# A two-layer adaLN transformer on one core: the expert stage with another order on TensorE, VectorE and GpSimd, GpSimd's own Newton steps, four sum and two output buffers

## The chip, the cores and the metric

One NeuronCore of a Trainium2 chip (trn2) runs the whole program. The metric is the device time of one execution in microseconds (us), the median of several runs; lower is better.

## What is computed

Two transformer layers with adaptive layer norm on x [8, 512, 256]. The change touches the last stage alone, in which the second layer's attention output is projected and normed and goes through a block of eight experts. Cut to that stage, with m the modulation rows (`ga`, `sb`, `cb`, `gb`) of a batch element:

```python
proj = (einsum('bhtk,hkd->bhtd', out_norm, Wo) + bo) * clip(gate, 0, 1)   # out_norm: by head
x = x + ga * proj.sum(axis=1) / H
h = layernorm(x) * (1 + cb) + sb
# the expert block, on h as [4096, 256]
x_attn = (layernorm(h) * ln_g + ln_b) @ attn_w + attn_b + h
g = x_attn.reshape(2, 8, 256, 256)                    # expert e takes 2 x 256 tokens
a = gelu(einsum('metd,edf->metf', g, w1) + b1)        # 256 -> 1024
y = einsum('metf,efd->metd', a, w2) + b2              # 1024 -> 256
x = x + gb * gelu(y @ next_w + next_b)
```

Every product is made from float16 halves: a high half and a low half of each operand, three matmuls for one product.

## The kernel before

The program has stages one after the other: attention and MLP of layer one, attention of layer two, and the stage of the change, `experts` (tile names with `D_`). It treats eight experts of 512 tokens each. Every engine walks the same list of ten bodies (`bodies`): body b works on three experts at once, e = b + 1 (projection of the attention output, sum, both norms), a = b (gate and the first expert product) and m = b - 1 (second expert product, last product, output). Engines take their instructions in the order in which the code writes them; between engines stand semaphores.

The names, in the order in which an expert goes through them:

- `project` (TensorE) multiplies yh, yl by the attention output weights into X; VectorE scales that into the sum buffer x3 (L2086), GpSimd adds the input rows x2t (L1860). x3 has three buffers, taken in turn.
- `statistics` (VectorE) takes mean and variance of the 512 tokens into mv and ve. `root_of` makes rstd = 1/sqrt(ve): a first guess r0 on GpSimd by the power -0.5 (L1845) and one Newton step, three instructions on VectorE (L2050, L2052, L2055). There are two roots for each expert: one for ht (L2094, L2099, four passes each), one for xn (L2108, four passes).
- `turn` (TensorE) transposes ht and xn through X. ScalarE copies them out (hTb, h2h), VectorE makes the low half h2l (L2119).
- `gate` (TensorE, 12 matmuls) multiplies h2h, h2l by attn_w; VectorE adds hTb (gf, L2074), ScalarE makes gh, GpSimd the low half gl (L1853).
- `first` (TensorE, s = 0 to 7, 6 matmuls each) fills PA; ScalarE makes af and Hh of it, VectorE the low half Hl (L2065, `splits`).
- `second` (TensorE, four chunks c of 12 matmuls) fills PW. ScalarE makes y2f and y2h, GpSimd y2l (L1865). `last` is the last product; ScalarE's gelu writes it to the output buffer xo (one buffer, the tile `last`), GpSimd's `finish` (L1835, L1838) multiplies by gb and adds x3, SyncE stores it.
- `weights` makes the float16 halves of an expert's weights, eh on ScalarE and el on VectorE (L2034), in two halves of w_st; half 0 is w1, half 1 is w2. SyncE loads the next half when the el of the one before is made. `prepare` makes yh (ScalarE) and yl (GpSimd, L1827) of the expert after next.

On TensorE body b issues: second(c=0), gate, second(c=1), project(q=0), second(c=2), project(q=1), second(c=3), first(0, 1), last, first(2, 3, 4), turn of ht, first(5, 6, 7), turn of xn. All matmuls of the expert products and the gate have one line, L2148; those of `project` and `last` have L2156 and L2160, the transposes L2207.

Of the kernel before, what the change touches and what calls it, by code (L numbers as in the profile page):

```python
# [21 lines left out]
TT = T // 128  # L22
# [1218 lines left out]
def mlp0(nc, d, keep, stay):  # L1241

    table = mlp_slots()
    with ExitStack() as ctx:
# [11 lines left out]
        ve, lnr, rstd = stay("ve", [128, TT]), stay("lnr", [128, 3, TT]), stay("rstd", [128, TT])  # L1256
        off = {"w1": 0, "w2": FT * HID, "h1": 2 * FT * HID, "h2": (2 * FT + HM) * HID, "w3": (2 * FT + 2 * HM) * HID}
# [415 lines left out]
def experts(nc, d, keep):  # L1673

    NA = HM
    with ExitStack() as ctx:
# [24 lines left out]
        x3 = [sb(f"x3{k}", [128, TT, C]) for k in range(3)]  # L1701
# [12 lines left out]
        xo = by_token(keep["last"])  # L1714
# [19 lines left out]
        n_mm, of_s, og_s, x4_s, o_st = sem("n_mm"), sem("of"), sem("og"), sem("x4"), sem("o_st")  # L1734
# [13 lines left out]
        def _(sp):  # L1748
# [46 lines left out]

            def body(b, e, a, m):
                n = b + 2
                if n < E8:
                    if n >= 2:
                        load_x(n)  # L1800
                    if n % 2 == 0 and n >= 4:
                        load_rows(n // 2)
                    load_w(n, 0)
                if m is not None:
                    q0, q1, t_ = halves(m)
                    for q_, q in enumerate((q0, q1)):
                        sp.wait_ge(x4_s, 2 * m + q_ + 1)
                        sp.dma_start(d["out"][q, t_, :].rearrange("(t p) c -> p t c", p=128),
                                     xo[:, 2 * q_:2 * q_ + 2, :]).then_inc(o_st, 16)
                if n < E8:  # L1810
                    load_w(n, 1)

            bodies(body)
            sp.wait_ge(o_st, 32 * E8)

        @block.gpsimd
        def _(pool):
# [12 lines left out]
            def finish(m):  # L1830

                for q in range(2):
                    v = xo[:, 2 * q:2 * q + 2, :]
# [4 lines left out]
                    nc.gpsimd.tensor_tensor(v, v, x3[m % 3][:, 2 * q:2 * q + 2, :], ALU.add).then_inc(x4_s, 1)  # L1838

            def root_of(nth):  # L1840

                pool.wait_ge(ve_s, nth + 1)
                if nth >= 1:
                    pool.wait_ge(newton, 3 * nth)
                nc.gpsimd.tensor_tensor(r0[:, :], ve[:, :], power[:, :], ALU.pow).then_inc(guess, 1)  # L1845

            prepare(0)

            def body(b, e, a, m):
# [26 lines left out]
        def _(act):  # L1876
# [58 lines left out]
            def body(b, e, a, m):  # L1935
# [52 lines left out]
        def _(dve):  # L1988
# [49 lines left out]
            def statistics(src, nth, ready):  # L2038
# [10 lines left out]
                dve.wait_ge(guess, nth + 1)  # L2049
# [288 lines left out]
```

## Time and profile before

| | us |
|---|---|
| median of 3 runs | 2118.07 |
| lowest and highest | 2112.24, 2121.11 |
| the profiled execution, its own time | 2117.34 |
| its span, first to last instruction | 2115.6 |
| PE (TensorE matmul) busy | 1862.5 (88%) |
| DVE (VectorE) busy | 1341.4 (63%) |
| ACT (ScalarE) busy | 1209.5 (57%) |
| POOL (GpSimd) busy | 577.1 (27%) |

The expert stage is the last sixth of the span. Moments in the trace are us from the span's start. "Busy" of PE overstates, since matmuls are pipelined and their records overlap. In a row of the timeline the first number is the start, the second how long the instruction or the merged run took; what stands in brackets is how long the engine had been idle before it and which instruction ended that.

### The profile page before, as it was taken

How to read it: one execution, taken by the hardware profiler on the slowest of the kernel's cores; microseconds unless marked ns; L12 is line 12 of the kernel's file. 1: busy time of each engine (PE TensorE's matmuls, PEld its weight loads, DVE VectorE, ACT ScalarE, POOL GpSimd, SP SyncE). 2: the span in 40 equal slices, each digit the busy share in tenths (PEclk: the TensorE clock that was granted, in tenths of full speed). 3: DMA queues.
4: the chain of work that ended last, by engine and by line, in shares of the span. 5: the costliest groups of instructions: out<-in, count | busy, mean ns of one | idle time of the engine just before them, and what ended most of it. 6: DMA issues, size and time to landing. Idle time of an engine off the chain costs nothing. (4 is left out here: it accounts for less than half of the span.)

```text
span 2115.6 us, 29755 instructions
## 1 busy us (share of the span) xinstructions
PE 1862.5 (88%) x10573; PEld 764.4 (36%) x10573; DVE 1341.4 (63%) x2591; ACT 1209.5 (57%) x1686; POOL 577.1 (27%) x668
## 2 busy tenths in 40 slices
PE   5789999988879999999899987899999884888887
PEld 3323332322234444444444432223333222444443
DVE  5478888888743553553444525888887854776771
ACT  4378887776742432433333424888888773565563
POOL 5666667671210000000001112111111002344443
PEclk8589999999999999999999996999999995999999
DMA  3344554344360000000010032233333305233210
GB/s 111 60 94 116 135 122 115 101 118 104 101 228 11 11 21 9 13 21 1 22 46 1 21 51 57 44 71 71 69 63 58 54 11 205 80 110 140 70 40 20
DMA packets 111987, 147.93 MB, mean 70 GB/s; under 512 B 11874, under 2 KB 95188, under 8 KB 109780
## 3 DMA queue, kind: packets, MB, share of 16 engines
q1 hardware_dynamic: 111828, 145.77, 25.8%
q8 instruction: 105, 1.72, 0.4%
q14 instruction: 54, 0.44, 0.1%
HBM read 100.34 MB, written 45.14 MB: 69 GB/s over the span
## 5 line engine op out<-in xcount | busy, mean ns | idle before, releaser
L825 DVE TENSOR_REDUCE A_M<-A_SM 128x1 f16<-128x512 f32 x1024 | 653.8, 685 | 183.2 <-PE A_SM L1034 180.9
L585 ACT ACTIVATE A_P<-A_ST 128x1024 f32<-128x1024 f32 x512 | 523.5, 1025 | 128.9 <-PE A_ST L1050 126.4
L1034 PE MATMUL A_SM<-A_KT,A_QS 48*128 48x512 f16 x1024 | 351.9, 400 | 57.8 <-DVE A_M L825 51.5
L1577 PE MATMUL B_PA<-B_Hh,B_wh 128*128 128x512 f16 x1024 | 388.1, 379 | 0.0
L1577 PE MATMUL B_PA<-B_Hl,B_wh 128*128 128x512 f16 x1024 | 388.1, 379 | 0.0
L1496 ACT ACTIVATE B_af<-B_PA,B_sv 128x512 f32<-128x512 f32 x192 | 131.9, 687 | 357.1 <-PE B_PA L1577 356.9
L1050 PE MATMUL A_ST<-A_QS,A_KT 49*128 49x512 f16 x1024 | 302.0, 388 | 0.2
L1067 PE MATMUL A_AV<-A_P,A_V 128*32 128x512 f32 x2048 | 281.2, 613 | 5.3 <-ACT A_P L585 4.8
L1034 PEld LDWEIGHTS A_SM<-A_KT,A_QS 48*128 48x128 f16 x1024 | 82.3, 94 | 434.9 <-DVE A_M L825 376.0
L1540 DVE TENSOR_SCALAR B_Hh<-B_af 128x512 f16<-128x512 f32 x128 | 58.3, 456 | 281.9 <-ACT B_af L1496 281.9
L1291 POOL TENSOR_TENSOR B_hl<-B_hf,B_hh 128x512 f16<-128x512 f32 x14 | 16.2, 1156 | 525.2 <-ACT B_hh L1307 525.2
L1577 PEld LDWEIGHTS B_PA<-B_Hl,B_wh 128*128 128x128 f16 x1024 | 100.2, 98 | 118.9
L1577 PEld LDWEIGHTS B_PA<-B_Hh,B_wh 128*128 128x128 f16 x1024 | 100.2, 98 | 118.7
L1542 DVE SCALAR_TENSOR_TENSOR B_Hl<-B_af,B_Hh 128x512 f16<-128x512 f32 x128 | 88.6, 692 | 4.4
L551 POOL TENSOR_TENSOR A_tr<-A_qkf,A_tr 128x512 f16<-128x512 f32 x28 | 32.4, 1156 | 155.0 <-ACT A_tr L681 155.0
L1534 DVE SCALAR_TENSOR_TENSOR B_uf<-B_PD,B_sv,B_af 128x512 f32<-128x512 f32 x64 | 47.8, 747 | 35.7 <-PE B_PD L1577 27.7
L1496 ACT ACT_TABLE_LOAD x23 | 29.5, 1283 | 66.9 <-PE B_PA L1577 55.0
L1067 PEld LDWEIGHTS A_AV<-A_P,A_V 128*32 128x32 f32 x2048 | 44.3, 108 | 62.8 <-issue 50.2
L937 PE MATMUL A_X<-A_wh,A_hh 128*128 128x256 f16 (+1 forms) x160 | 52.5, 328 | 9.9 <-ACT A_V L629 7.4
L1050 PEld LDWEIGHTS A_ST<-A_QS,A_KT 49*128 49x128 f16 x1024 | 55.7, 94 | 14.4 <-ACT A_P L585 12.2
L1577 PE MATMUL B_PA<-B_hh,B_wh 128*128 128x512 f16 x128 | 50.8, 397 | 9.8 <-issue 9.8
L2065 DVE SCALAR_TENSOR_TENSOR D_Hl<-D_af,D_Hh 128x512 f16<-128x512 f32 x64 | 45.9, 752 | 17.2 <-ACT D_Hh L1931 17.2
(338 smaller groups left out, 3275.1 us busy)
## 6 DMA issues: line engine op xcount, KB each, us to landing
D_w_st<-in_we_dram SPq DMA_DIRECT2D x16, 1024.0 KB, 4.8
qk<-A_tr SPq DMA_DIRECT2D x58, 256.0 KB, 2.4
A_KT<-qk SPq DMA_DIRECT2D x96, 128.0 KB, 4.8
A_QS<-qk SPq DMA_DIRECT2D x96, 128.0 KB, 5.1
A_w_st<-in_w_ffn_dram SPq DMA_DIRECT2D x32, 352.0 KB, 3.6
w_hi<-A_f_hi SPq DMA_DIRECT2D x32, 176.0 KB, 3.6
w_lo<-A_f_lo SPq DMA_DIRECT2D x32, 176.0 KB, 3.8
B_wl<-w_lo SPq DMA_DIRECT2D x1, 5632.0 KB, 23.0
```

What stands on the lines that cost most here:

```text
L585: nc.scalar.activation(P[:, st, 2 * pair:2 * pair + 2, :], ST[:, u % 2, :, :], ACT.Exp, scale=1.0 / math.sqrt(HD)).then_inc(exp_s, 1)
L825: nc.vector.tensor_reduce(M[G % 2][:, tt, o:o + 1], SM[:, n % 2, :], AX, ALU.max, negate=True).then_inc(max_s, 1)
L937: ins = nc.tensor.matmul(out, a, c, start=first and n_ == 0, stop=last and n_ == len(todo) - 1)
L1034: nc.tensor.matmul(SM[:, n % 2, :], QS[b % 2][r, 2 * g + pair, tt * 128:tt * 128 + 128], KT[b % 2][r, 2 * g + pair, :], start=True, stop=T ...
L1050: ins = nc.tensor.matmul(ST[:, u % 2, a, :], KT[b % 2][r, pair, o:o + 128], QS[b % 2][r, pair, :], start=True, stop=True)
L1067: ins = nc.tensor.matmul(AV[32 * j:32 * j + 32, :], V[b % 3][:, st, g * HG + j, :], P[:, st, j, :], start=st == 0, stop=st == TT - 1)
L1496: nc.scalar.activation(af[:, s % 3, :], PA[:, s % 4, :], ACT.Silu if s < HM else ACT.Gelu, scale=sv[:, which, m:m + 1]).then_inc(a_out, 1)
L1534: nc.vector.scalar_tensor_tensor(out=uf[:, s % 2, :], in0=PD[:, s % 2, :], scalar=sv[:, 1, s:s + 1], in1=src, op0=ALU.mult, op1=ALU.mult). ...
L1540: nc.vector.tensor_scalar(Hh[w][:, m, :], src, HS, None, ALU.mult).then_inc(high, 1)
L1542: nc.vector.scalar_tensor_tensor(out=Hl[w][:, m, :], in0=src, scalar=HS, in1=Hh[w][:, m, :], op0=ALU.mult, op1=ALU.subtract).then_inc(spli ...
L1577: ins = nc.tensor.matmul(out, a, c, start=start and kt == 0 and n_ == 0, stop=stop and kt == kts[-1] and n_ == len(ops) - 1)
L2065: nc.vector.scalar_tensor_tensor(out=Hl[:, s, :], in0=af[:, s % 4, :], scalar=HS, in1=Hh[:, s, :], op0=ALU.mult, op1=ALU.subtract).then_in ...
```

## The change

Seven things are written differently, all in `experts`; nothing that is computed changes, but for the form of the Newton step.

1. TensorE: the gate stands behind chunk 1 of `second` and not behind chunk 0; the two halves of `project` behind chunks 2 and 3, not 1 and 2.
2. The Newton step is made by GpSimd, right behind the power: four instructions on 128x4 instead of three on VectorE, which waits for the fourth only where it uses rstd: ahead of the second half of ht and ahead of xn.
3. GpSimd's order in a body: `finish` now serves the expert before m and stands right behind gl; y2l stands between the two sums; both roots stand one behind the other, `prepare` behind them. The last expert is finished at the end of its own body.
4. VectorE: el of half 0 stands between the second statistics and xn, not ahead of the sums.
5. x3 has four buffers; the fourth lies in a tile of an earlier stage (`B_xT0`).
6. xo has two buffers; the second lies in a tile of an earlier stage (`B_wh0`); each has a semaphore for its stores.
7. SyncE stores expert m - 1 in the body of m, behind the load of the weights' half 0, which waits for el of half 0 as before.

```diff
@@ buffers
-        x3 = [sb(f"x3{k}", [128, TT, C]) for k in range(3)]
+        x3 = [sb(f"x3{k}", [128, TT, C]) for k in range(3)] + [by_token(keep["spare"])]
...
-        xo = by_token(keep["last"])
+        other = keep["spare2"][:, 0:TT * C * 2].bitcast(F32).rearrange("p (t c) -> p t c", t=TT)
+        xo = [by_token(keep["last"]), other]
@@ sync, body
                     load_w(n, 0)
...
+                if m is not None and m >= 1:
+                    store(m - 1)
                 if n < E8:
                     load_w(n, 1)
+                if m == E8 - 1:
+                    store(m)
@@ gpsimd
             def root_of(nth):
 
+                k = 4 * nth
                 pool.wait_ge(ve_s, nth + 1)
-                if nth >= 1:
-                    pool.wait_ge(newton, 3 * nth)
                 nc.gpsimd.tensor_tensor(r0[:, :], ve[:, :], power[:, :], ALU.pow).then_inc(guess, 1)
+                pool.wait_ge(guess, nth + 1)
+                nc.gpsimd.tensor_tensor(rt[:, :], r0[:, :], r0[:, :], ALU.mult).then_inc(newton, 1)
+                pool.wait_ge(newton, k + 1)
+                nc.gpsimd.tensor_tensor(rt[:, :], rt[:, :], ve[:, :], ALU.mult).then_inc(newton, 1)
+                pool.wait_ge(newton, k + 2)
+                nc.gpsimd.tensor_scalar(rt[:, :], rt[:, :], -0.5, 1.5, ALU.mult, ALU.add).then_inc(newton, 1)
+                pool.wait_ge(newton, k + 3)
+                nc.gpsimd.tensor_tensor(rstd[:, :], rt[:, :], r0[:, :], ALU.mult).then_inc(newton, 1)
...
+                if m is not None and m >= 1:
+                    finish(m - 1)
+                for q in range(2):
+                    if e is not None:
+                        add_tokens(e, q)
+                    if m is not None and q == 0:
+                        for f in range(FT):
+                            pool.wait_ge(y2_out, FT * m + f + 1)
+                            nc.gpsimd.tensor_tensor(y2l[:, f, :], y2f[:, f, :], y2h[:, f, :], ALU.subtract).then_inc(y2_low, 1)
                 if e is not None:
...
                     root_of(2 * e)
...
                     root_of(2 * e + 1)
-                if m is not None:
-                    finish(m)
                 if b + 2 < E8:
                     prepare(b + 2)
+                if m == E8 - 1:
+                    finish(m)
@@ vector
-                dve.wait_ge(guess, nth + 1)
-                nc.vector.tensor_tensor(rt[:, :], r0[:, :], r0[:, :], ALU.mult).then_inc(newton, 1)
...
-                dve.wait_ge(newton, 3 * nth + 3)
...
-                    if e >= 3:
-                        dve.wait_ge(x4_s, 2 * (e - 2))
-                    weights(e, 0)
+                    if e >= 4:
+                        dve.wait_ge(x4_s, 2 * (e - 3))
...
+                    dve.wait_ge(newton, 4 * (2 * e) + 4)
...
                     statistics(ht, 2 * e + 1, lambda tt: dve.wait_ge(h_s, TT * e + tt + 1))
+                    weights(e, 0)
                     if e >= 1:
                         dve.wait_ge(td_mm, FT * e)
+                    dve.wait_ge(newton, 4 * (2 * e + 1) + 4)
@@ tensor, body
                     if m is not None:
                         second(m, c)
-                    if a is not None and c == 0:
+                    if a is not None and c == 1:
                         gate(a)
-                    if e is not None and c in (1, 2):
-                        project(e, c - 1)
+                    if e is not None and c in (2, 3):
+                        project(e, c - 2)
```

Three places in the engines' order. Lines of the changed kernel are some 10 to 20 higher for the same instruction.

GpSimd, one middle body from gl on, before (`D_r` is the power, `last` the output buffer):

```order
L1853 TENSOR_TENSOR D_gl<-D_gf,D_gh 128x512 x2
L1860 TENSOR_TENSOR D_x<-D_x,D_x2t 128x512 x2
L1845 TENSOR_TENSOR D_r<-D_ve,D_power 128x4
L1865 TENSOR_TENSOR D_y2l<-D_y2f,D_y2h 128x512 x2
L1845 TENSOR_TENSOR D_r<-D_ve,D_power 128x4
L1835 TENSOR_TENSOR last<-last,D_rows 128x512
L1838 TENSOR_TENSOR last<-last,D_x 128x512
```

and the same body in the changed kernel, up to the first root (here the sum lies in `B_xT`):

```order
L1878 TENSOR_TENSOR D_gl<-D_gf,D_gh 128x512 x2
L1845 TENSOR_TENSOR last<-last,D_rows 128x512
L1848 TENSOR_TENSOR last<-last,D_x 128x512
L1845 TENSOR_TENSOR last<-last,D_rows 128x512
L1848 TENSOR_TENSOR last<-last,D_x 128x512
L1856 TENSOR_TENSOR B_xT<-B_xT,D_x2t 128x512
L1887 TENSOR_TENSOR D_y2l<-D_y2f,D_y2h 128x512 x2
L1856 TENSOR_TENSOR B_xT<-B_xT,D_x2t 128x512
L1862 TENSOR_TENSOR D_r<-D_ve,D_power 128x4
L1864 TENSOR_TENSOR D_rt<-D_r 128x4
```

The four passes of `finish` moved from the end of the body to a place ahead of the sums, y2l went between the sums, and behind the power stand the steps.

VectorE from the second statistics to xn and what follows, before:

```order
L2048 TENSOR_SCALAR D_ve<-D_mv 128x4
L2050 TENSOR_TENSOR D_rt<-D_r 128x4
L2052 SCALAR_TENSOR_TENSOR D_rt<-D_rt,D_ve 128x4
L2055 SCALAR_TENSOR_TENSOR D_rstd<-D_rt,D_r 128x4
L2108 TENSOR_SCALAR D_xn<-D_ht,D_mv,D_rstd 128x256 x4
L2065 SCALAR_TENSOR_TENSOR D_Hl<-D_af,D_Hh 128x512 x3
```

and in the changed kernel:

```order
L2071 TENSOR_SCALAR D_ve<-D_mv 128x4
L2057 SCALAR_TENSOR_TENSOR D_el<-D_w_st,D_eh 128x1024 x2
L2124 TENSOR_SCALAR D_xn<-D_ht,D_mv,D_rstd 128x256 x4
L2079 SCALAR_TENSOR_TENSOR D_Hl<-D_af,D_Hh 128x512 x3
L2057 SCALAR_TENSOR_TENSOR D_el<-D_w_st,D_eh 128x1024 x2
```

The three steps are gone from VectorE, and two el passes stand between ve and xn, where GpSimd makes the root.

TensorE where the last chunk of `second` ends, before (`D_PA` is `first`):

```order
L2148 MATMUL D_PW<-D_Hh,D_eh 128x512
L2148 MATMUL D_PW<-D_Hl,D_eh 128x512
L2148 MATMUL D_PW<-D_Hh,D_el 128x512
L2148 MATMUL D_PA<-D_gh,D_eh 128x512
L2148 MATMUL D_PA<-D_gl,D_eh 128x512
L2148 MATMUL D_PA<-D_gh,D_el 128x512
```

and in the changed kernel:

```order
L2164 MATMUL D_PW<-D_Hh,D_eh 128x512
L2164 MATMUL D_PW<-D_Hl,D_eh 128x512
L2164 MATMUL D_PW<-D_Hh,D_el 128x512
L2172 MATMUL D_X<-D_row,D_ones 128x256
L2176 MATMUL D_X<-D_wsh,D_yh 128x256
L2176 MATMUL D_X<-D_wsh,D_yl 128x256
```

The second half of `project` stands behind that chunk now, and `first` behind it; the gate has moved by one chunk in the same way.

## Rows read from the trace of the kernel before

**Rows 1.** Page, chain that ended last, its shares of the span by engine:

```profile
DVE 9%; PE 4%; POOL 2%; issue 2%; DMA 1%; ACT 0%; SPq 0%; POOLq 0%; ACTq 0%; DVEq 0%
```

**Rows 2.** Windows from gate to gate: length, PE, PEld, DVE, ACT, POOL busy, clock, DMA:

```profile
1822.60:1863.17 40.57, 34.98 (x181) 17.39 (x181) 29.31 (x57) 23.24 (x36) 16.84 (x15) 0.96 0.25 88
...
1903.74:1942.63 38.89, 33.29 (x181) 16.98 (x181) 28.58 (x57) 23.74 (x37) 17.22 (x15) 1.00 0.28 96
...
2023.78:2064.36 40.58, 34.97 (x180) 17.36 (x180) 29.30 (x57) 20.98 (x32) 16.37 (x14) 0.96 0.08 30
```

**Rows 3.** Timeline of TensorE, from one gate to the next:

```profile
1903.74 0.39 PE L2148 MATMUL D_X<-D_h2h,D_wsh 128*128 128x512 f16 x1 [2.65 <-DVE D_h2l L2119]
...
1906.34 0.38 PE L2148 MATMUL D_PW<-D_Hh,D_eh 128*128 128x512 f16 x1
...
1922.44 0.28 PE L2156 MATMUL D_PW<-D_row,D_ones 2*128 2x256 f16 x1 [1.69 <-POOL D_y2l L1865]
...
1936.15 1.09 PE L2207 MATMUL D_X<-id,D_xn 128*128 128x128 f32 x8 [1.11 <-DVE D_xn L2108]
...
1942.63 0.60 PE L2148 MATMUL D_X<-D_h2h,D_wsh 128*128 128x512 f16 x1 [2.79 <-DVE D_h2l L2119]
```

**Rows 4.** Timeline of VectorE in the same body:

```profile
1915.61 0.69 DVE L2086 SCALAR_TENSOR_TENSOR D_x<-D_X,D_rows 128x512 f32<-128x512 f32 x1 [3.67 <-PE D_X L2160]
...
1917.68 0.75 DVE L2042 BATCH_NORM_STATS2 D_st<-D_x 128x6 f32<-128x256 f32 x2 [0.72 <-POOL D_x L1860]
...
1922.64 1.67 DVE L2094 SCALAR_TENSOR_TENSOR D_ht<-D_x,D_mv,D_rows 128x256 f32<-128x256 f32 x4
...
1925.81 1.29 DVE L2065 SCALAR_TENSOR_TENSOR D_Hl<-D_af,D_Hh 128x512 f16<-128x512 f32 x2
...
1930.15 1.23 DVE L2050 TENSOR_TENSOR D_rt<-D_r 128x4 f32<-128x4 f32 x1 [1.12 <-POOL D_r L1845]
...
1932.77 3.32 DVE L2108 TENSOR_SCALAR D_xn<-D_ht,D_mv,D_rstd 128x256 f32<-128x256 f32 x4
...
1937.82 2.35 DVE L2034 SCALAR_TENSOR_TENSOR D_el<-D_w_st,D_eh 128x1024 f16<-128x1024 f32 x2
...
1941.30 1.27 DVE L2119 TENSOR_TENSOR D_h2l<-D_X,D_h2h 128x512 f16<-128x512 f32 x2
```

**Rows 5.** Timeline of GpSimd in the same body:

```profile
1906.68 2.45 POOL L1853 TENSOR_TENSOR D_gl<-D_gf,D_gh 128x512 f16<-128x512 f32 x2 [0.26 <-ACT D_gh L1939]
...
1919.13 1.02 POOL L1845 TENSOR_TENSOR D_r<-D_ve,D_power 128x4 f32<-128x4 f32 x1 [1.49 <-DVE D_ve L2048]
1920.12 2.26 POOL L1865 TENSOR_TENSOR D_y2l<-D_y2f,D_y2h 128x512 f16<-128x512 f32 x2
...
1930.09 1.27 POOL L1835 TENSOR_TENSOR last<-last,D_rows 128x512 f32<-128x512 f32 x1
```

**Rows 6.** Timeline of VectorE in the first body, GpSimd idle:

```profile
1784.96 0.16 DVE L2055 SCALAR_TENSOR_TENSOR D_rstd<-D_rt,D_r 128x4 f32<-128x4 f32 x1
1785.16 1.38 DVE L2108 TENSOR_SCALAR D_xn<-D_ht,D_mv,D_rstd 128x256 f32<-128x256 f32 x4
```

**Rows 7.** Timeline of ScalarE, the body of rows 3:

```profile
1918.79 0.68 ACT L1951 ACTIVATE D_y2h<-D_PW,D_eb 128x512 f16<-128x512 f32 x1
```

**Rows 8.** Timeline of GpSimd in the second attention, a root by the same steps:

```profile
1503.60 1.04 POOL L459 TENSOR_TENSOR A_lnr<-A_ve,A_power 128x4 f32<-128x4 f32 x1
...
1505.56 0.20 POOL L448 TENSOR_TENSOR A_rstd<-A_lnr 128x4 f32<-128x4 f32 x1
```

**Rows 9.** Timelines, GpSimd and VectorE near 1201, VectorE near 1943:

```profile
1200.77 0.64 POOL L448 TENSOR_TENSOR A_rstd<-A_lnr 128x4 f32<-128x4 f32 x1
...
1200.66 0.69 DVE L1542 SCALAR_TENSOR_TENSOR B_Hl<-B_af,B_Hh 128x512 f16<-128x512 f32 x1
...
1942.49 1.36 DVE L2065 SCALAR_TENSOR_TENSOR D_Hl<-D_af,D_Hh 128x512 f16<-128x512 f32 x1
```

**Rows 10.** Page, DMA issues: count, KB each, us from issue to landing:

```profile
D_w_st<-in_we_dram SPq DMA_DIRECT2D x16, 1024.0 KB, 4.8
```

More of the change, by code:

```diff
@@ L1256, in mlp0 @@
         ve, lnr, rstd = stay("ve", [128, TT]), stay("lnr", [128, 3, TT]), stay("rstd", [128, TT])
+        keep["spare"], keep["spare2"] = xT[0], wh0
         off = {"w1": 0, "w2": FT * HID, "h1": 2 * FT * HID, "h2": (2 * FT + HM) * HID, "w3": (2 * FT + 2 * HM) * HID}
@@ L1733, in experts @@
         w2_mm, y2_s, y2_out, y2_low = sem("w2_mm"), sem("y2_s"), sem("y2_out"), sem("y2_low")
-        n_mm, of_s, og_s, x4_s, o_st = sem("n_mm"), sem("of"), sem("og"), sem("x4"), sem("o_st")
+        n_mm, of_s, og_s, x4_s = sem("n_mm"), sem("of"), sem("og"), sem("x4")
+        o_st = [sem(f"o_st{k}") for k in range(2)]
         block = ctx.enter_context(nc.Block())
@@ L1794, in _, with store @@
             load_rows(1)
+            def store(m):
+                q0, q1, t_ = halves(m)
+                for q_, q in enumerate((q0, q1)):
+                    sp.wait_ge(x4_s, 2 * m + q_ + 1)
+                    sp.dma_start(d["out"][q, t_, :].rearrange("(t p) c -> p t c", p=128),
+                                 xo[m % 2][:, 2 * q_:2 * q_ + 2, :]).then_inc(o_st[m % 2], 16)
             def body(b, e, a, m):
@@ L1803, in body @@
                     load_w(n, 0)
-                if m is not None:
[L1805 to L1809, printed above, removed]
+                if m is not None and m >= 1:
+                    store(m - 1)
                 if n < E8:
                     load_w(n, 1)
+                if m == E8 - 1:
+                    store(m)
             bodies(body)
-            sp.wait_ge(o_st, 32 * E8)
+            for k in range(2):
+                sp.wait_ge(o_st[k], 32 * E8 // 2)
         @block.gpsimd
@@ L2086, in body @@
                         nc.vector.scalar_tensor_tensor(
-                            out=x3[e % 3][:, 2 * q:2 * q + 2, :], in0=X[:, q, :].rearrange("p (t c) -> p t c", t=2),
+                            out=x3[e % 4][:, 2 * q:2 * q + 2, :], in0=X[:, q, :].rearrange("p (t c) -> p t c", t=2),
                             scalar=1 / WS, in1=R[:, q, GA, :].unsqueeze(1).to_broadcast([128, 2, C]),
                             op0=ALU.mult, op1=ALU.mult).then_inc(z_sc, 1)
-                    statistics(x3[e % 3], 2 * e, lambda tt: dve.wait_ge(x3_s, 2 * e + tt // 2 + 1))
+                    statistics(x3[e % 4], 2 * e, lambda tt: dve.wait_ge(x3_s, 2 * e + tt // 2 + 1))
                     if e >= 1:
```

38 lines of the change are left out of this document (13 added, 25 removed).

## Prediction

> **What bounds the kernel now.** First the chain that ended last [rows 1]: of its engine shares VectorE's is the largest, and its lines are those of the expert stage. The edits touch that stage alone, so I read only it, body by body from one gate to the next [rows 2]. Of the six full bodies, from the gate at 1822.60 on, one takes 38.89 us and the other five 40.57 or 40.58. A body holds some 35 us of matmul records but 29 of VectorE and 17 of GpSimd: TensorE carries most, but waits. Its waits in a body [rows 3]: 1.7 for the low halves of y2 ahead of `last`, 1.1 for xn ahead of the second transposes, 2.7 to 2.8 for h2l ahead of the gate. The granted clock is 0.96 in a 40.57 body and 1.00 in the 38.89 one [rows 2]: in the others a stretch at the lower level (1.2 instead of 2.4 GHz) follows a wait of TensorE, in [rows 3] the gate's matmuls take 0.60 instead of 0.39 behind one of 2.79. That is 40.57 - 38.89 = 1.7 us.
>
> What TensorE waits for is one loop: gate, gl, projections, sums, first root, ht, second root, xn, h2l, next gate. On VectorE [rows 4] the last stretch of it is dear for a reason: a Newton step takes 1.23 us and the four xn passes 3.32, while GpSimd runs y2l or `finish` [rows 5]; where GpSimd is idle, a step takes 0.16 and xn 1.38 [rows 6]. So the two engines keep each other out.
>
> I write all moments as us after a gate's start g, from the full-clock body (g = 1903.74).
>
> **TensorE's order.** The gate takes 1906.34 - 1903.74 = 2.60 [rows 3], a chunk of `second` the same less 0.01 (12 matmuls like the gate's). A second chunk ahead of the gate covers 2.59 of the 2.8 wait. Behind the gate, chunk and projection still alternate: the second product of the projection lands at g + 11.9 as before (1915.61 [rows 4]). With no wait left, the work between gates is 40.57 - 2.8 - 1.7 - 1.1 less 1.7 for the clock, some 33: I take 32.8, **the floor of a body**.
>
> **GpSimd's order.** gl ends at g + 5.4 [rows 5]. Then `finish` of the expert before, four passes of 1.27 and hops, 5.2: to 10.6. Before, it came last and nothing of the loop stood behind it; now the first sum does (1.27, to 11.9), y2l (2.26, to 14.2) and the second sum (to 15.5). The statistics add 0.75 (1917.68) and 0.7 of small ones: ve at **17.0**, where the first root's start, 1919.13, puts it at 15.3 before. `finish` thus costs 1.7 there. In exchange y2l ends at 14.2, when TensorE has done its two stages of `first` (11.7 + 2.6), so the 1.7 wait goes: ScalarE's last y2h ended at 1919.47 [rows 7], g + 15.7 and 1.4 after the last chunk (11.7 + 2.6); that chunk now ends at 9.7, so y2h is there at 11.2.
>
> **The roots.** GpSimd has done these very four steps elsewhere: from the start of the power to the end of the last step 1505.56 + 0.20 - 1503.60 = 2.16 us, each step 0.20 and a hop of 0.08 [rows 8]. Unheld, rstd stands 2.2 after ve. It will not be unheld: behind ve VectorE now goes straight on, with four ht passes (1.67) at the first root and two el passes (2.35) at the second, all with two operands in SBUF. One such pass held a step of GpSimd for 0.64 instead of 0.20, to 0.06 after its own end (1200.66 + 0.69 = 1201.35, against 1201.41) [rows 9]; the other way, Hl took 1.36 beside a yl pass, twice a free one (1.29 for two [rows 4]). Nothing shows a power beside such a pass, so from both sides: no hold, 2.2 and 2.2; result written only when the passes are done, 1.7 + 1.2 = 2.9 and 2.4 + 1.2 = 3.6; the whole power started only then, 3.9 and 4.6. A power written between the passes gives 2.6 and 3.3. I take the middle of that and of the second, **2.75 and 3.45**, since the held step fits these best.
>
> Here the Trainium skill speaks (GPSIMD Engine Reference, Key points): GpSimd shares its SBUF interfaces with VectorE and meets instructions with two SBUF inputs, and VectorE is about twice as fast for elementwise work. The first half the trace bears out with 0.64 for 0.20; by the second the steps should not have moved, and by it alone each would cost twice 0.16, a root 0.6 more than with unheld steps on VectorE. Beside a GpSimd pass the trace says otherwise, 1.23 against 0.20.
>
> **One body, walked.** ve 17.0; rstd 19.75; the second half of ht 1.65 to 21.4, before TensorE asks for it (22.0); two Hl 1.2 to 22.6; statistics 1.95 (from the end of the Hl, 1927.10, to that of ve, 1930.15 - 1.12 = 1929.03 [rows 4]) to 24.55; rstd 28.0 (the el passes end at 26.9 and are hidden); xn 1.38 to 29.4. TensorE wants xn at 26.75: **a wait of 2.7 takes the place of the three**. From the end of xn to h2l there are three Hl, two el, two Hl, two h2l: 1942.57 - 1936.09 = 6.5, so the next gate stands at **g + 35.95**. TensorE's own way, transposes 0.87 and two chunks 5.18, is 6.1, 0.4 less. With a lower-clock stretch behind the 2.7 wait that way is 1.7 longer, and the gate 1.3 later: 37.2. Five of six bodies show such a stretch now; two in three gives **36.8**.
>
> Sum, against the profiled execution:
> - Bodies before the first full one. No `finish` there, but both experts pay the held roots: each second root with xn now takes 3.45 + 1.4 = 4.85 where a power of 1.0, three steps of 0.16 [rows 6], hops and xn's 1.38 made 3.1, each first one saves 0.55, and el no longer stands ahead of the sums of expert 1 (up to 2.35, I take 1.95). 2 x 1.75 - 2 x 0.55 - 1.95 = **+0.5**.
> - Body 1: no `finish` yet, so ve is at 15.3: 34.3 instead of 40.57, **-6.3**.
> - Bodies 2 to 6: 2 x 40.57 + 38.89 + 2 x 40.58 = 201.2; now 5 x 36.8 = 184.0: **-17.2**.
> - From the last gate to the end, 2115.6 - 2064.36 = 51.3. One chunk less stands behind the gate (-2.6), its clock dip goes (-1.6), y2l now stands behind a `finish` until 12.95 where `last` wants it at 10.4 (+2.6), and that wait may bring a dip (+0.7): **-0.9**.
> - Weight loads: half 0 is asked for only after the moved el passes, at g + 26.9; it lands in 4.8 [rows 10] and is wanted at g' + 4, some 13 later. Stores leave a body later, into two buffers, with a body to land. Sum buffers: the sum that is waited for was finished a body before. At nothing; if the load took over 13, its excess would come on each body.
>
> Together -23.9: 2117.34 - 23.9 = 2093.4. The median of the three runs is 0.7 above the profiled execution's time, so **2094**.
>
> **Rivals.**
> - *No hold.* Roots of 2.2: xn is bound by the el passes (2.4), g + 34.3, a TensorE wait of 1.1 and no dips. 2.5 less in five bodies, 1.5 in body 1, some 3 outside: 2117.3 - 41 = 2076. For it: the steps of [rows 8] all stay at 0.20. Against: [rows 9]. 0.20.
> - *Whole hold.* 3.9 and 4.6: 2.3 more for each of eight experts, 18, and the wait of TensorE at 5 with a dip each time: 2111. For it: Hl waited for a whole pass. Against: four elements a partition read little. 0.15.
> - *Dear steps, slower.* If a step on GpSimd cost here what the power costs (1.04) and not 0.20, eight steps for each of eight experts add 64 x 0.84 = 54: 2147. The gain is gone at 0.20 + 23.9 / 64 = 0.57 a step, and the kernel slower by over 0.5% from 0.74 on. For it: the held step's 0.64, if all were held so, ends at 2121. Against: by the time of most steps VectorE has run out of passes and waits. 0.05.
> - *The wait only moves.* The changed order does what it says, but if `last`, ht and xn shift so that TensorE loses as much ahead of the transposes as it wins at the gate, nothing is left: 2117. It needs a wait of 40.57 - 32.8 = 7.8 there, and is the upper end of the whole hold. 0.05.
>
> **How the numbers follow.** Forecast as walked, 2085 to 2103 by its ends (35.95 and 37.2 a body, roots up to the second bound): 0.55. With 0.20, 0.15, 0.05 and 0.05 that is all. The range reaches to the no-hold case and, on the other side, into the whole hold: **2070 to 2110**. A difference of 0.5% (10.6 us) is about what a measurement of this kernel tells from none. Faster by more, under 2107.5: 0.55 + 0.20 + a third of the whole hold and of the rest, 0.82; within: 0.11; slower: 0.07.
>
> **What would show it.** Gates 36 to 37 apart, and 34 in body 1; no wait ahead of the gate over 0.5, none ahead of `last`, one of 2 to 3 before the second transposes; rstd 2.6 to 2.9 and 3.3 to 3.6 after ve, with steps lengthened only while ht or el passes run; xn at 1.4; `finish` right behind gl and the first sum from g + 10.7. Wrong would be: rstd at 2.2 (then 2076), a power of 2 us or more (then 2111), sums that wait for the table of rows or for a buffer, or a TensorE that waits longer than 3 at the transposes.

## The result, and the profile after

The changed kernel takes 2089.17 us (median of five runs, 2084.33 to 2089.56), the kernel before beside it 2113.36 (five runs, 2110.61 to 2121.11): a ratio of 0.9875, with a 95% interval of 0.9856 to 0.9894. The profiled execution took 2089.56, its span is 2087.9 (before: 2117.34 and 2115.6). One execution of the late-pass experiment below took 2241.01 at a granted clock of 0.82, where its others show 0.95, and is left out of that experiment's time.

Windows from gate to gate (columns as in [rows 2]), of the changed kernel: body 1, body 2, body 5, and from the last gate to the end.

```profile
1827.64:1861.45 33.81, 33.21 (x181) 16.96 (x180) 21.20 (x50) 23.26 (x36) 13.38 (x18) 1.00 0.23 77
1861.45:1896.59 35.14, 33.23 (x180) 16.95 (x181) 22.44 (x51) 23.25 (x36) 19.54 (x23) 1.00 0.40 135
...
1966.88:2002.04 35.16, 33.22 (x180) 16.98 (x181) 22.45 (x51) 23.25 (x36) 19.55 (x23) 1.00 0.32 105
...
2037.19:2087.90 50.71, 38.06 (x188) 18.05 (x188) 10.13 (x11) 18.87 (x30) 22.38 (x18) 0.92 0.09 32
```

Against [rows 2] each of bodies 2 to 6 is 5.4 (one of them 3.7) shorter, VectorE is busy 6 to 7 us less in it, and the granted clock is 1.00 in all. TensorE's waits in the body of the gate at 1966.88, to compare with [rows 3] (`last` starts at 1981.24 without a wait):

```profile
1966.88 0.39 PE L2164 MATMUL D_X<-D_h2h,D_wsh 128*128 128x512 f16 x1 [0.20 <-DVE D_h2l L2135]
1995.56 0.44 PE L2223 MATMUL D_X<-id,D_xn 128*128 128x128 f32 x2 [1.73 <-DVE D_xn L2124]
```

Three waits of 5.5 in all have become 1.9. GpSimd in that body, against [rows 5]; the power is the row with D_r:

```profile
1969.82 2.46 POOL L1878 TENSOR_TENSOR D_gl<-D_gf,D_gh 128x512 f16<-128x512 f32 x2 [0.69 <-ACT D_gh L1962]
1972.23 1.27 POOL L1845 TENSOR_TENSOR B_wh<-B_wh,D_rows 128x512 f32<-128x512 f32 x1
...
1977.39 1.27 POOL L1856 TENSOR_TENSOR D_x<-D_x,rare 128x512 f32<-128x512 f32 x1
1978.61 2.27 POOL L1887 TENSOR_TENSOR D_y2l<-D_y2f,D_y2h 128x512 f16<-128x512 f32 x2
1980.84 1.27 POOL L1856 TENSOR_TENSOR D_x<-D_x,rare 128x512 f32<-128x512 f32 x1
1983.60 1.18 POOL L1862 TENSOR_TENSOR D_r<-D_ve,D_power 128x4 f32<-128x4 f32 x1 [1.49 <-DVE D_ve L2071]
1984.86 0.29 POOL L1864 TENSOR_TENSOR D_rt<-D_r 128x4 f32<-128x4 f32 x1
...
1990.93 1.91 POOL L1862 TENSOR_TENSOR D_r<-D_ve,D_power 128x4 f32<-128x4 f32 x1 [4.93 <-DVE D_ve L2071]
```

and VectorE, against [rows 4]:

```profile
1983.43 1.66 DVE L2107 SCALAR_TENSOR_TENSOR D_ht<-D_x,D_mv,D_rows 128x256 f32<-128x256 f32 x4
1986.04 1.67 DVE L2113 SCALAR_TENSOR_TENSOR D_ht<-D_ht,D_rstd,D_rows 128x256 f32<-128x256 f32 x4 [0.94 <-POOL D_rstd L1870]
...
1990.76 2.35 DVE L2057 SCALAR_TENSOR_TENSOR D_el<-D_w_st,D_eh 128x1024 f16<-128x1024 f32 x2
1994.12 1.38 DVE L2124 TENSOR_SCALAR D_xn<-D_ht,D_mv,D_rstd 128x256 f32<-128x256 f32 x4 [1.01 <-POOL D_rstd L1870]
```

`finish` stands right behind gl, the sums and y2l without a gap behind it; the first power is held a little, the second by 0.9; xn takes 1.38 instead of 3.32 but waits 1.01 for rstd.

Where the 27.7 us of the span went: up to the second gate +5.0 (1827.64 for 1822.60), body 1 -6.8, bodies 2 to 6 -25.4 (175.74 for 201.19), the rest -0.5. Of the first, 4.1 lies ahead of the stage: its first product starts at 1771.00 instead of 1766.88. I take that moment not to be the change's: over the profiled executions of all kernels here, which are alike up to there, it lies between 1759.8 and 1772.1. From the first product to the end, the stage takes 348.7 in the trace of the kernel before and 316.9 here, 31.8 less; by the ratio of the medians the gain is 26 (22 to 30). So below I compare bodies first, and the whole by its median.

### The profile page after: what moved, and what is told of

Same layout as the page of the kernel before. It is cut to its first block and busy times, and to the rows that moved or that the text cites. A ratio compares the mean times of both kernels' runs of the same rounds, so it can differ in the third digit from the quotient of the medians.

```text
span 2087.9 us, 29755 instructions
## 1 busy us (share of the span) xinstructions
PE 1855.1 (89%) x10573; PEld 763.2 (37%) x10573; DVE 1300.7 (62%) x2543; ACT 1210.4 (58%) x1686; POOL 600.4 (29%) x732
## 5 line engine op out<-in xcount | busy, mean ns | idle before, releaser
L1535 DVE SCALAR_TENSOR_TENSOR B_uf<-B_PD,B_sv,B_af 128x512 f32<-128x512 f32 x64 | 47.8, 747 | 35.9 <-PE B_PD L1578 27.7
L1949 ACT ACTIVATE D_af<-D_PA,D_eb 128x512 f32<-128x512 f32 x64 | 43.7, 683 | 28.7 <-PE D_PA L2164 17.4
L1578 PE MATMUL B_PA<-B_hh,B_wh 128*128 128x512 f16 x128 | 50.4, 394 | 10.2 <-issue 10.2
```

Of the source, the lines that this page charges most:

```text
L1535: nc.vector.scalar_tensor_tensor(out=uf[:, s % 2, :], in0=PD[:, s % 2, :], scalar=sv[:, 1, s:s + 1], in1=src, op0=ALU.mult, op1=ALU.mult). ...
L1578: ins = nc.tensor.matmul(out, a, c, start=start and kt == 0 and n_ == 0, stop=stop and kt == kts[-1] and n_ == len(ops) - 1)
L1949: nc.scalar.activation(af[:, s % 4, :], PA[:, s % 4, :], ACT.Gelu, bias=eb[:, a, s:s + 1], scale=1 / WS).then_inc(a_out, 1)
```

## The experiments

My theory after the result: TensorE's order pays because a chunk covers the wait for h2l; GpSimd's pays because steps and xn no longer run beside its passes; what is left, 1.73, is the held roots. The rival for the first: a cover that only moves the wait. All ratios are to the kernel before, run beside them on the same chip, with the 95% interval.

**TensorE's old order in the changed kernel**

```diff
-                    if a is not None and c == 1:
+                    if a is not None and c == 0:
                         gate(a)
-                    if e is not None and c in (2, 3):
-                        project(e, c - 2)
+                    if e is not None and c in (1, 2):
+                        project(e, c - 1)
```

> The changed kernel with TensorE's old order alone: gate behind chunk 0 of second, the halves of project behind chunks 1 and 2. Theory (the loop through VectorE and GpSimd sets the body, not TensorE): the next gate still stands 6.54 us behind the end of xn, and TensorE reaches the second transposes 2.6 later than now, where it now waits 1.73 for xn, so a body stays near 35.2 but for up to 1 us at the transposes; the wait of some 3 us in front of the gate is back and with it stretches at the lower clock, 1.7 each. 2090 to 2100, and the wait in front of the gate 2.5 to 3. Rival (the cover of a chunk is worth what it covers): each of seven bodies pays 2.6, plus the dips: 2107 or more.

Measured: 2106.43 (six runs), 0.9936 (0.991 to 0.9961), bodies of 38.1, two of 39.7 and 39.8; TensorE waits 1.11 or 2.80 ahead of the gate and 2.00 ahead of the transposes. The old order costs a body 3 and more, where I expected it to stay near 35.2, and the reason is another than mine. GpSimd in the body of the gate at 1903.75:

```profile
1914.24 1.26 POOL L1856 TENSOR_TENSOR D_x<-D_x,rare 128x512 f32<-128x512 f32 x1
1918.26 2.45 POOL L1887 TENSOR_TENSOR D_y2l<-D_y2f,D_y2h 128x512 f16<-128x512 f32 x2 [2.76 <-ACT D_y2h L1974]
1920.67 1.26 POOL L1856 TENSOR_TENSOR D_x<-D_x,rare 128x512 f32<-128x512 f32 x1
```

and VectorE behind it:

```profile
1921.96 0.75 DVE L2065 BATCH_NORM_STATS2 D_st<-D_x 128x6 f32<-128x256 f32 x2 [5.00 <-POOL D_x L1856]
```

The last chunk of `second` ends 2.6 later, so y2l does too, and with GpSimd's new order the second sum is queued behind y2l: the statistics come 3 us later.

**TensorE's new order alone in the kernel before** (the same lines, the other way round)

> The kernel before with TensorE's new order alone: gate behind chunk 1 of `second`, project behind chunks 2 and 3; all other engines as before. Theory: the loop gate, gl, projections, sums, roots, xn, h2l, gate does not hold the chunks of `second`, so it stays as long as it was; the 2.8 us of wait ahead of the gate only move to a place ahead of the transposes or of `last`. Bodies of 38.9 to 40.6, 2106 to 2117. Rival, what the prediction's first step says by itself: the chunk covers 2.6 us of wait, bodies of 37.5 to 38, 2098 to 2102.

Measured: 2111.83 (ten runs), 0.9985 (0.9967 to 1.0003), bodies of 38.9, 39.5 and two of 41.3 (above the expected 40.6; the clock in those two is 0.88). No wait is left ahead of the gate or the transposes; there is one of 4.28 ahead of `last`. Timeline of TensorE in the body of the gate at 1907.65:

```profile
1926.34 0.39 PE L2156 MATMUL D_PW<-D_row,D_ones 2*128 2x256 f16 x1 [4.28 <-POOL D_y2l L1865]
```

ScalarE's last y2h in it, and then GpSimd:

```profile
1918.15 0.68 ACT L1951 ACTIVATE D_y2h<-D_PW,D_eb 128x512 f16<-128x512 f32 x1
```

```profile
1923.03 1.02 POOL L1845 TENSOR_TENSOR D_r<-D_ve,D_power 128x4 f32<-128x4 f32 x1 [1.49 <-DVE D_ve L2048]
1924.02 2.26 POOL L1865 TENSOR_TENSOR D_y2l<-D_y2f,D_y2h 128x512 f16<-128x512 f32 x2
```

y2h is there at 1918.83, but GpSimd makes y2l of it only 5.2 later, behind the second sum and the root. The wait has moved, as this theory said, and the whole can't be told from the kernel before. In the traces little is left of the gain: the six full bodies take 239.4 together instead of 241.8, and the stretch behind the last gate, with one chunk less in it, 47.0 instead of 51.2. In the bodies TensorE's order needs GpSimd's to be worth more than 0.4.

**TensorE's old order, and y2l behind the first root** (in the changed kernel; it takes the coupling of the first experiment away)

> The changed kernel with TensorE's old order (gate behind chunk 0 of `second`, project behind chunks 1 and 2), as in e1_pe_back, and with the two y2l passes of GpSimd not between the two sums but behind the first root. Theory: in e1 the 3 us a body went lost because y2h comes 2.6 us later by that order and the second sum stands behind y2l on GpSimd. With y2l out of its way the second sum ends at g + 13.9, ve stands at g + 15.3 instead of 19.6, and the body is bound by VectorE again: 35 to 36.5 instead of 38.1, in all 2088 to 2100. Rival: the order of TensorE costs by itself, by the wait ahead of the gate with its lower-clock stretch; then the body stays at 37.5 or more, 2104 or more.

Measured: 2118.58 (ten runs), 1.0015 (0.9996 to 1.0034), bodies of 39.6 and 42.3 by turns. ve came at g + 15.3 as expected, and the rest of the theory fell. TensorE from the gate at 1898.62 on:

```profile
1898.62 0.39 PE L2165 MATMUL D_X<-D_h2h,D_wsh 128*128 128x512 f16 x1 [1.80 <-DVE D_h2l L2136]
1918.86 0.28 PE L2173 MATMUL D_PW<-D_row,D_ones 2*128 2x256 f16 x1 [3.24 <-POOL D_y2l L1889]
```

GpSimd and, behind it, VectorE there:

```profile
1916.36 2.44 POOL L1889 TENSOR_TENSOR D_y2l<-D_y2f,D_y2h 128x512 f16<-128x512 f32 x2
```

```profile
1916.44 3.43 DVE L2114 SCALAR_TENSOR_TENSOR D_ht<-D_ht,D_rstd,D_rows 128x256 f32<-128x256 f32 x4 [0.94 <-POOL D_rstd L1870]
```

y2l is late for `last` again (3.24), TensorE then never waits for xn, and still waits 1.80 for h2l: between the transposes and h2l lie 4.4 us of ScalarE and VectorE, and one chunk covers 2.6 of them. VectorE is not what is late there: it sits idle for 1.03 ahead of h2l, until ScalarE's h2h has come. So in this kernel 1.8 is TensorE's own gain from the second chunk ahead of the gate. 32.9 + 3.2 + 1.8 and a lower-clock stretch of 1.7 is 39.6; the bodies of 42.3 show the same waits and 2.7 more of busy TensorE, at a clock of 0.88 instead of 0.96. Note also ht: 3.43 beside y2l, 1.67 free.

**`finish(m)` at the body's end again**, behind the roots, as before; all else as changed

```diff
-                if m is not None and m >= 1:
-                    finish(m - 1)
...
                     root_of(2 * e + 1)
+                if m is not None:
+                    finish(m)
...
-                if m == E8 - 1:
-                    finish(m)
```

> The changed kernel with finish at its old place, for expert m behind both roots (Newton steps stay on GpSimd). Theory (the place of finish is the gain, through what it does to VectorE): ve is 1.3 earlier, but the four finish passes meet the xn passes, xn takes 3.3 or more instead of 1.38, a body 36.5 to 37 and TensorE waits over 3 ahead of the transposes, with dips: 2098 to 2108. Rival (GpSimd's passes in front of the sums only delay ve, and the Newton steps are the gain): a body of 33.9, 2081.

Measured: 2108.64 (ten runs), 0.9963 (0.9946 to 0.9981), bodies of 38.7 and 39.8. ve comes 1.3 earlier as expected, but xn now meets `finish`, and that costs more than the 36.5 to 37 a body that I expected. GpSimd and, behind it, VectorE:

```profile
2010.42 1.27 POOL L1845 TENSOR_TENSOR last<-last,D_rows 128x512 f32<-128x512 f32 x1
```

```profile
2010.58 5.21 DVE L2122 TENSOR_SCALAR D_xn<-D_ht,D_mv,D_rstd 128x256 f32<-128x256 f32 x4 [1.00 <-POOL D_rstd L1870]
```

5.21 instead of 1.38: the four xn passes last as long as the four of `finish` beside them (2010.42 to 2015.64), so each seems to wait for one. TensorE's wait ahead of the transposes is 4.2 (1.73 in the changed kernel), and a stretch at the lower clock follows it (0.96 or 0.91). Of the parts taken back one by one, the place of `finish` is the dearest, about 4 us a body.

**el of half 0 ahead of the sums again**

```diff
+                    weights(e, 0)
                     for q in range(2):
                         dve.wait_ge(z_mm, 2 * e + q + 1)
...
                     statistics(ht, 2 * e + 1, lambda tt: dve.wait_ge(h_s, TT * e + tt + 1))
-                    weights(e, 0)
```

> The changed kernel with el of half 0 on VectorE at its old place, ahead of the sums. Theory (VectorE instructions with two SBUF operands and GpSimd passes keep each other out, both ways): the power of the second root takes 1.02 instead of 1.91 and xn starts 2.3 behind ve instead of 3.27, but el now meets finish, whose four passes end up to 2.3 later, and so does ve: a body 35.2 to 36.5, 2090 to 2098. Rival (el only fills idle time of VectorE there): 0.9 less in each body, 2082.

Measured: 2091.3 (four runs), 0.9881 (0.9854 to 0.9907), bodies of 36.0. The second power is free and takes 1.01, but el and `finish` now hold each other, and the sums behind them come 1.8 later. GpSimd and, behind it, VectorE in the body of the gate at 1929.46:

```profile
1934.81 2.25 POOL L1845 TENSOR_TENSOR last<-last,D_rows 128x512 f32<-128x512 f32 x1
1937.14 2.13 POOL L1848 TENSOR_TENSOR last<-last,D_x 128x512 f32<-128x512 f32 x1
...
1955.31 1.01 POOL L1862 TENSOR_TENSOR D_r<-D_ve,D_power 128x4 f32<-128x4 f32 x1 [4.93 <-DVE D_ve L2071]
```

```profile
1934.67 3.47 DVE L2057 SCALAR_TENSOR_TENSOR D_el<-D_w_st,D_eh 128x1024 f16<-128x1024 f32 x2 [1.71 <-ACT D_eh L1938]
```

The move of el is worth 0.9 a body, though the whole can't be told from the changed kernel's; the hold of the second power is the smaller of two prices.

**The hold, measured**: el of half 0 in four passes of 512 columns

```diff
-                    nc.vector.scalar_tensor_tensor(out=el[e % 2][:, half, o:o + HID], in0=w_st[:, half, o:o + HID],
...
+                    n = 2 - half
+                    for i in range(n):
+                        p = slice(o + i * HID // n, o + (i + 1) * HID // n)
+                        ins = nc.vector.scalar_tensor_tensor(out=el[e % 2][:, half, p], in0=w_st[:, half, p],
...
+                    ins.then_inc(e_low, 1)
```

> The changed kernel with el of half 0 in four passes of 512 columns instead of two of 1024 between ve and xn; all else as it is. Theory, read from the changed kernel's roots: a power of GpSimd is held until the VectorE pass that runs at its start has ended, and takes 0.9 from there, whatever follows. Its first pass now ends about 0.6 earlier, so the second power takes 1.3 to 1.4 instead of 1.91; a step behind it may be held by a pass of 0.6 once or twice; the root from ve to rstd 2.6 to 2.9 instead of 3.17, bodies of 34.6 to 34.9, 2085 to 2088. Rival: the power waits for all passes that stand queued (then 3.3 or more), or its hold does not depend on the pass (then 1.91 as now); bodies of 35.15 or more, 2089 or more.

Measured: 2087.54 (four runs), 0.985 (0.9801 to 0.9898), bodies of 35.0. GpSimd and, behind it, VectorE from the second ve (end 1989.85) on:

```profile
1989.93 1.38 POOL L1862 TENSOR_TENSOR D_r<-D_ve,D_power 128x4 f32<-128x4 f32 x1 [4.93 <-DVE D_ve L2075]
1991.38 0.32 POOL L1864 TENSOR_TENSOR D_rt<-D_r 128x4 f32<-128x4 f32 x1
1991.78 0.52 POOL L1866 TENSOR_TENSOR D_rt<-D_rt,D_ve 128x4 f32<-128x4 f32 x1
```

```profile
1989.76 2.49 DVE L2060 SCALAR_TENSOR_TENSOR D_el<-D_w_st,D_eh 128x512 f16<-128x512 f32 x4
```

The power fell from 1.91 to 1.38, as the theory's 1.3 to 1.4; two of the steps were held in turn (0.32 and 0.52), so the root fell from 3.17 to 3.02 only, and the body by 0.16. The root (2.6 to 2.9) and the body (34.6 to 34.9) missed what was expected by 0.1, and the whole can't be told from the changed kernel's.

**Three sum buffers instead of four**

```diff
-        x3 = [sb(f"x3{k}", [128, TT, C]) for k in range(3)] + [by_token(keep["spare"])]
+        x3 = [sb(f"x3{k}", [128, TT, C]) for k in range(3)]
...
-                    if e >= 4:
-                        dve.wait_ge(x4_s, 2 * (e - 3))
+                    if e >= 3:
+                        dve.wait_ge(x4_s, 2 * (e - 2))
```

> The changed kernel with three sum buffers instead of four; all else as it is. VectorE's scaling of the first product of experts 3 to 7 then has to wait until `finish` of the expert three before has added its sum, at g + 10.5, where it now stands at g + 7.4. Theory: the first sum of GpSimd starts 0.8 later, at g + 11.3, everything behind it too, and the five bodies that are concerned last 35.9 to 36.0 instead of 35.15: 2093 to 2094. Rival: the scaling of the second product and the statistics take the delay up, and nothing changes: 2089.

Measured: 2092.7 (four runs), 0.9898 (0.9856 to 0.9941), bodies of 36.0 to 36.1, two of 37.4. Below are VectorE at the first scaling and the windows of two bodies.

```profile
1901.21 0.69 DVE L2099 SCALAR_TENSOR_TENSOR D_x<-D_X,D_rows 128x512 f32<-128x512 f32 x1 [7.12 <-POOL B_wh L1848]
```

```profile
1890.59:1926.68 36.09, 33.29 (x181) 17.00 (x181) 22.55 (x51) 23.24 (x36) 19.55 (x23) 1.00 0.32 102
1926.68:1964.03 37.35, 34.81 (x181) 17.52 (x182) 23.76 (x51) 23.24 (x36) 20.87 (x24) 0.95 0.41 142
```

The scaling waits for `finish`, and the body is 0.9 longer, as worked out. The fourth buffer is what lets `finish` stand ahead of the sums at its price. The second window shows the same waits with a lower-clock stretch: 1.3.

**The Newton step on VectorE again**

```diff
...
                 nc.gpsimd.tensor_tensor(r0[:, :], ve[:, :], power[:, :], ALU.pow).then_inc(guess, 1)
-                pool.wait_ge(guess, nth + 1)
-                nc.gpsimd.tensor_tensor(rt[:, :], r0[:, :], r0[:, :], ALU.mult).then_inc(newton, 1)
...
-                    dve.wait_ge(newton, 4 * (2 * e) + 4)
+                    step(2 * e)
...
-                    dve.wait_ge(newton, 4 * (2 * e + 1) + 4)
+                    step(2 * e + 1)
```

(`step` holds the three instructions of the kernel before, L2049 to L2057.)

> The changed kernel with the Newton step back on VectorE as three instructions, asked for where the changed kernel waits for rstd; GpSimd makes the power alone. Theory (the steps were dear on VectorE only because finish ran beside them): each step takes 0.16 to 0.2, the second half of ht starts 2.27 behind ve instead of 2.52, xn 2.86 instead of 3.27, a body is 34.5 instead of 35.15, and the kernel some 5 us faster than the changed one, 2084. Rival (GpSimd's own steps are what brought the gain): steps of 1.1 again, some 2 us a body, 2100 or more.

Measured: 2076.8 (four runs), 0.981 (0.9786 to 0.9834), bodies of 34.2 (34.5 was expected). The window of a middle body, then GpSimd's second power and, behind it, the step on VectorE:

```profile
1950.55:1984.73 34.18, 33.22 (x181) 16.96 (x181) 23.23 (x57) 23.25 (x36) 17.79 (x15) 1.00 0.34 108
```

```profile
1974.13 1.91 POOL L1863 TENSOR_TENSOR D_r<-D_ve,D_power 128x4 f32<-128x4 f32 x1 [5.71 <-DVE D_ve L2064]
```

```profile
1976.23 0.15 DVE L2069 TENSOR_TENSOR D_rt<-D_r 128x4 f32<-128x4 f32 x1
1976.42 0.16 DVE L2071 SCALAR_TENSOR_TENSOR D_rt<-D_rt,D_ve 128x4 f32<-128x4 f32 x1
1976.61 0.16 DVE L2074 SCALAR_TENSOR_TENSOR D_rstd<-D_rt,D_r 128x4 f32<-128x4 f32 x1
```

Once no GpSimd pass runs beside it, a step costs VectorE 0.16, and no hop between the engines is needed: 0.4 and 0.5 less for the two roots. Moving the step to GpSimd was a loss of 1 us a body within the change. The whole is 7 below what was expected and, by the two ratios, some 14 below the changed kernel, of which the six full bodies give 6. The rest is not explained; in this trace the stage starts at 1759.8, the earliest of all.

**The second sum ahead of y2l's second half**

```diff
                     if e is not None:
                         add_tokens(e, q)
-                    if m is not None and q == 0:
-                        for f in range(FT):
-                            pool.wait_ge(y2_out, FT * m + f + 1)
-                            nc.gpsimd.tensor_tensor(y2l[:, f, :], y2f[:, f, :], y2h[:, f, :], ALU.subtract).then_inc(y2_low, 1)
+                    if m is not None:
+                        pool.wait_ge(y2_out, FT * m + q + 1)
+                        nc.gpsimd.tensor_tensor(y2l[:, q, :], y2f[:, q, :], y2h[:, q, :], ALU.subtract).then_inc(y2_low, 1)
```

> The changed kernel with GpSimd's order first sum, y2l of half 0, second sum, y2l of half 1, instead of first sum, both y2l, second sum. The second sum then ends 1.1 us earlier, ve at g + 15.5, and by VectorE's way the next gate stands 1.1 earlier; y2l is complete at g + 15.2 where `last` asks for it at g + 14.3, a wait of 0.9 on TensorE, after which the second transposes wait 0.7 or less. Theory: bodies of 34.1 to 34.3 instead of 35.15, 2083 to 2085. Rival: the new wait of TensorE comes on top, 36.0 and 2093.

Measured: 2081.04 (four runs), 0.9839 (0.9798 to 0.9879), bodies of 34.03, both a little under what was expected; the wait for xn is gone, one of 0.85 stands ahead of `last`. The two waits are in one chain, so one takes the other's place and does not come on top.

**A late pass of `finish`, early y2l at the end**: with the step on VectorE, the fourth pass of `finish` stands behind the first root and waits for Hl of s = 1; where a body has no sum, y2l (`low_half`) stands ahead of `finish`. The diff without that of the step:

```diff
+                early = m is not None and e is None and a is not None
+                late = m is not None and m >= 1 and e is not None
+                if early:
+                    low_half(m)
                 if m is not None and m >= 1:
-                    finish(m - 1)
+                    finish(m - 1, (0, 1, 2) if late else (0, 1, 2, 3))
...
                     root_of(2 * e)
+                    if late:
+                        pool.wait_ge(split, NA * a + 2)
+                        finish(m - 1, (3,))
                     root_of(2 * e + 1)
```

> The changed kernel with the Newton step on VectorE (as in e2_newton_ve), and two moves on GpSimd: the fourth pass of `finish` stands behind the first root and waits for Hl of s = 1, so that it runs beside the statistics of the second norm; and in the last body but one, which has no sum, y2l stands ahead of `finish`. Theory: the first sum starts 1.3 earlier, y2l at once when y2h is there, ve at g + 15.6; statistics are not held by a GpSimd pass, so the second root starts about 0.8 earlier than in e2 and the wait of 0.75 ahead of the second transposes goes; bodies of 33.4 instead of 34.2, and the wait of 2.7 in the last body but one goes: 2068 to 2071. Rival: the moved pass delays the second power or holds the ht passes or el as it did in e3_finish_last; bodies of 34.2 or more, 2073 to 2080.

Measured: 2071.5 (2063.68 to 2073.88 in three runs), 0.9786 (0.9735 to 0.9838), the lowest time here, with bodies 0.5 shorter than expected. The window of a middle body, then GpSimd's late pass and VectorE's statistics beside it:

```profile
1956.08:1988.97 32.89, 32.89 (x181) 17.03 (x181) 22.56 (x57) 23.18 (x37) 17.55 (x14) 1.00 0.34 113
```

```profile
1976.43 1.27 POOL L1846 TENSOR_TENSOR B_wh<-B_wh,B_xT 128x512 f32<-128x512 f32 x1 [3.77 <-DVE D_Hl L2102]
```

```profile
1976.27 1.40 DVE L2076 BATCH_NORM_STATS2 D_st<-D_ht 128x6 f32<-128x256 f32 x4
```

A body is 32.89 and TensorE busy for all of it: no wait is left, and this is the floor for this amount of matmul work at the full clock. The moved pass and the statistics run beside each other at their free lengths. The last stretch is 47.9 instead of 50.7. The edit makes three moves at once; the next experiment takes one of them, the step, back.

**The same with the step on GpSimd** (the changed kernel with these two moves only)

> e8_late_pass with the Newton steps back on GpSimd: the changed kernel with the fourth pass of `finish` behind the first root and, in the last body but one, y2l ahead of `finish`, and nothing else. Theory: ve stands at g + 15.3 as in e8, both roots take the 0.4 and 0.6 longer that the changed kernel's took against e2_newton_ve, xn ends 1.0 later than in e8, at g + 27.3, where TensorE comes at g + 26.9: a wait of 0.4 to 0.5 ahead of the second transposes comes back, and by VectorE's way (6.5 from the end of xn) bodies last 33.7 to 33.9, one more than in e8; in all about 6 above e8, 2076 to 2080. Rival: where the late pass has given the roots room, the step's place costs nothing; bodies of 32.9, 2072.

Measured: 2074.83 (four runs), 0.9814 (0.9785 to 0.9843). The window of a middle body:

```profile
1961.03:1994.85 33.82, 33.22 (x180) 16.95 (x181) 22.45 (x51) 23.25 (x36) 19.57 (x23) 1.00 0.33 108
```

Its 33.82 is 0.93 above the last experiment's: the step's place costs its 1 us a body here too. The whole lies just under the expected range; its interval and that of the experiment before overlap.

## Why the prediction was right, step by step

The time, 2089, is 5 below the forecast of 2094 and in its range, and in the main the mechanism was the one forecast: the waits ahead of the gate and `last` went, xn ran free behind `finish`'s new place, and held roots left one wait ahead of the transposes. How near the number came is partly luck. The sum of -23.9 holds only terms of the stage, and in the traces the stage is 31.8 shorter, a third more; a later start of the stage took 4.1 of that back, and the two medians lie 24.2 apart.

| | forecast | measured |
|---|---|---|
| ve of the first norm | g + 17.0 | g + 16.64 |
| the two roots, ve to rstd | 2.75, 3.45 | 2.48, 3.17 |
| xn done | g + 29.4 | g + 28.62 |
| wait ahead of the second transposes | 2.7 | 1.73 |
| end of xn to the next gate | 6.5 | 6.54 |
| bodies 2 to 6 | 36.8 | 35.15 |
| body 1 | 34.3 | 33.81 |
| last gate to the end | 50.4 | 50.71 |
| ahead of the first full body | +0.5 | +0.9 in the stage, +4.1 ahead of it |
| floor of a body | 32.8 | 32.89 (late pass) |

- **The term that was mis-sized** is bodies 2 to 6: -25.4 for -17.2. Of the 1.65 a body, 0.8 is the end of xn (ve 0.4 and the two roots together 0.5 earlier, 0.1 of it lost again between them; I took the middle of two bounds, and the lower, 2.6 and 3.3, was nearer, since only the first VectorE pass holds the power and not the whole group), and 0.85 the lower-clock stretch, which I charged to two bodies in three: with a wait of 1.73 none showed it. So the signs that I had named, gates 36 to 37 apart, rstd 2.6 to 2.9 and 3.3 to 3.6 behind ve and a wait of 2 to 3, were all missed to the same side, by 0.1 to 0.9. The ends that I gave for the walked case, 2085 and 2103, are also wider than the terms named for them, which make some 2087 (with roots of 2.6 and 3.3) and 2098.
- **TensorE's order.** The waits ahead of the gate and `last` went as said, but "covers 2.59 of the 2.8" is only half the account: alone, it moves the wait ahead of `last` (ratio 0.9985). What it earns is 1.8 a body of its own (shown with y2l behind the root), and a y2h 2.6 earlier, which the new place of y2l needs. Order and place are one edit.
- **GpSimd's order.** That `finish` costs 1.7 ahead of the sums and frees steps and xn held: with it last, xn took 5.21 and a body 39.
- **The step's place.** This step of the forecast was wrong. It took the steps on GpSimd as part of the gain, by 1.23 against 0.20, the price of a VectorE step beside a GpSimd pass, which the same edit moves away. They are a loss of 1: beside no pass, three steps of 0.16 on VectorE beat four of 0.20 and their hops. The Trainium skill (GPSIMD Engine Reference, Key points) says that VectorE is the faster one for elementwise work. By 2.76 against 3.27 from the end of the second ve to xn (the step on VectorE, and the changed kernel) this case's runs agree, once the order is right, though a step less and shorter gaps between the steps are part of it.
- **Buffers.** With the fourth sum buffer no body waits for one; three cost 0.9 a body. w_st landed in 5.0 (median) and no full body waited for it. No run here takes the second output buffer away.

In the last body but one TensorE waits 2.73 for a y2l behind `finish`. I had it (+2.6), but not that y2l could stand first there.

## What to carry to other kernels

When two engines hold each other, first move the long passes of one to where the other is idle or does only what isn't held (here the scaling out of X, and for the late pass the statistics), and then give the short chain back to the engine that does it with fewer hops. A new order on the engine that carries most of the work is worth what the other engines' orders let through: change it alone and read where the wait went. Find the floor (a body with no wait) before pricing the parts; the last microseconds of this one came from moving single passes.

## What the runs showed of the hardware

- A GpSimd power on 128x4 is held until the VectorE pass with two SBUF operands that runs at its start is over, and ends 0.86 to 0.87 after that: 1.01 with no pass, 1.18 beside ht (passes of 0.48), 1.38 beside el of 512 columns (0.69), 1.91 beside el of 1024 (1.22). What follows the first pass does not lengthen it.
- Full passes of the two engines hold each other, and the times fit turns of one for one: four xn passes 5.21 for 1.38, ht 3.43 for 1.67, el 3.47 for 2.35, and `finish` 2.25 for 1.27. Statistics do not take part: 1.40 beside a GpSimd pass (above) and 1.40 with GpSimd idle, with the step on VectorE.
- The granted clock did not follow the sum of waits: 1.00 with 1.46 and 1.04 in a body (el early); 1.00 with 2.00 and 2.80, but 0.96 or 0.91 with 2.00 and 1.11 (TensorE's old order); and either 1.00 or 0.95 with 0.6 and 2.00 (three sums). From the last gate to the end it was 0.92 (changed kernel) or 0.83 (el in four passes) with the same wait of 2.7, and the stretch 50.7 or 55.1.
